# A four-phase graph network on one core: SyncE fetches one of 56 turns' rows in each GAT walk, and the index staging goes

## The reference, cut to what matters

```
def _gat_layer(x, src, dst, W, a_s, a_d, b, num_nodes):
    h = (x @ W).reshape(num_nodes, H, C)                     # H = 4, C = 32
    e = leaky_relu(alpha_src[src] + alpha_dst[dst], 0.2)
    e = exp(e - segment_max(e, dst)[dst])
    alpha = e / segment_sum(e, dst)[dst]
    return segment_sum(h[src] * alpha[:, :, None], dst) + b
```

## Time and profile before

| what | value |
|---|---|
| median of three runs | 6568.11 us |
| span of the profiled execution | 6570.3 us |
| VectorE busy | 4654.6 us, 71% |
| GpSimd busy | 4293.2 us, 65% |
| indirect gathers of rows (L725) | 3136, 2987.4 us busy |
| ScalarE busy | 1375.2 us, 21% |

### The profile page before, as it was taken

The page is one execution under the profiler, slowest core; times in us unless marked ns, Lnnn a source line. Parts: engine busy times, 40 slices in busy tenths (PEclk is TensorE's granted clock), DMA queues, the critical chain, the costliest instruction groups (busy, mean ns, idle before and its releaser), DMA issues. The chain is left out here.

```text
span 6570.3 us, 37158 instructions
## 1 busy us (share of the span) xinstructions
PE 1251.3 (19%) x8049; PEld 1094.3 (17%) x8049; DVE 4654.6 (71%) x9455; ACT 1375.2 (21%) x3580; POOL 4293.2 (65%) x4445
## 2 busy tenths in 40 slices
PE   7100000145555534332000000810000010000000
PEld 6100000135544433322000000610000010000000
DVE  7788888799999969987888887744444444444445
ACT  0122222220111114431000000622222211222223
POOL 0777777667777760027777775367777767777775
PEclk9555555555555555556555555955555555555555
DMA  9666666433443437754666664123333323333332
GB/s 391 199 218 202 202 199 204 130 106 131 132 136 133 133 115 292 295 184 153 220 219 218 225 218 158 30 85 109 113 111 109 115 74 90 112 113 109 113 111 82
DMA packets 338944, 1032.97 MB, mean 157 GB/s; under 512 B 100325, under 2 KB 163137, under 8 KB 331294
## 3 DMA queue, kind: packets, MB, share of 16 engines
q0 software_dynamic: 166752, 401.68, 21.4%
q1 hardware_dynamic: 116642, 342.34, 14.8%
q10 hardware_dynamic: 55324, 286.57, 12.1%
HBM read 602.97 MB, written 427.39 MB: 157 GB/s over the span
## 5 line engine op out<-in xcount | busy, mean ns | idle before, releaser
L725 POOL DMA_INDIRECT rows<-table,idx x3136 | 2987.4, 953 | 985.0 <-issue 973.1
L644 POOL DMA_INDIRECT by_src<-ebuf,place x784 | 767.4, 979 | 275.0 <-issue 238.3
L1296 DVE SCALAR_TENSOR_TENSOR psA<-psA,cont,dstf 128x128 f32<-128x128 f32 (+1 forms) x2349 | 836.6, 356 | 48.0 <-ACT ebuf L1025 27.2
L1285 DVE TENSOR_TENSOR sc<-rows,ebuf 128x56 f32<-128x56 f32 x112 | 28.2, 252 | 1023.9 <-DMA rows<-table,idx 1023.9
L958 PE MATMUL psA<-dstf,ones 128*128 128x512 f32 x10 | 9.9, 1113 | 3055.3 <-DVE dstf L2223 3055.3
L1296 DVE SCALAR_TENSOR_TENSOR sums<-sums,cont,psA 128x128 f32<-128x128 f32 (+1 forms) x1512 | 518.9, 343 | 30.3 <-ACT psA L1221 29.0
L958 PEld LDWEIGHTS psA<-dstf,ones 128*128 128x128 f32 x10 | 2.7, 317 | 3056.9 <-issue 3056.9
L823 PE MATMUL psA<-attr,sums 128*128 128x49 f32 x1568 | 406.1, 403 | 470.8 <-DVE attr L1475 470.8
L2104 DVE TENSOR_TENSOR_SCAN psA<-rows,psA 128x1980 f32<-128x1980 f32 x112 | 480.0, 4286 | 3.9
L823 PEld LDWEIGHTS psA<-attr,sums 128*128 128x128 f32 x1568 | 397.0, 326 | 476.9 <-DVE attr L1475 476.9
L1227 ACT ACTIVATE psA<-df 128x60 f32<-128x60 f32 (+1 forms) x168 | 40.4, 241 | 1714.2 <-DVE df L1285 1714.2
(11 more groups left out here) (350 smaller groups left out, 5533.6 us busy)
## 6 DMA issues: line engine op xcount, KB each, us to landing
dstf<-spread_wide SPq DMA_DIRECT2D x168, 924.0 KB
states<-sums ACTq DMA_DIRECT2D x150, 952.0 KB, 4.0
rows<-by_src SPq DMA_DIRECT2D x55, 1035.0 KB, 5.1
states<-sums ACTq DMA_DIRECT2D x56, 1008.0 KB, 5.7
spread_wide<-sums SPq DMA_DIRECT2D x56, 924.0 KB, 24.7
states<-sums ACTq DMA_DIRECT2D x56, 903.0 KB, 7.4
rows<-table,idx POOLq DMA_INDIRECT x3136
msg<-low_rows SPq DMA_DIRECT2D x56, 448.0 KB, 3.7
```

The source lines that it names most:

```text
L644: pool.indirect_dma_start(by_src[:, :], bass.IndirectOffsetOnAxis(ap=place[:, s, j:j + 1], axis=0), payload[:, s, j, :], None).then_inc(so ...
L725: pool.indirect_dma_start(rows[:, at:at + GW[ph]], None, table[ph][:, :], bass.IndirectOffsetOnAxis(ap=idx[:, s, j:j + 1], axis=0)).then_i ...
L1285: return dve.tensor_tensor(o_, a_, b_, op)
L1296: return dve.scalar_tensor_tensor(o_, a_, s_, b_, op0, op1)
```

## The change

In each GAT walk, turn 54 is left out of GpSimd's gathers. SyncE fetches its rows: for each of the 128 partitions it loads the 14 indices into registers, and for each index issues one copy of a single row of the table to its place in `msg`. VectorE reads turn 54 from `msg`, after a semaphore of its own. The other 55 turns of a GAT walk use the two slots of `rows` in turn, so turn 55 takes slot 0. In all four walks the staging of indices is gone: the gathers take their offsets from `src` directly, and POOL waits for `rows_used` alone.

```diff
+SIDE = {3: 54, 4: 54}
...
-        src = sb("src", [P, CH + 2 * B], I32)
+        src = sb("src", [P, CH], I32)
...
+        def row_slot(ph, g):
+            side = SIDE.get(ph, NG)
+            return None if g == side else (g - int(g > side)) % 2
+        def free_at(ph, g):
+            s = row_slot(ph, g)
+            users = [k for k in range(g) if row_slot(ph, k) == s]
+            return 2 + TURN[ph] * NG + (users[-1] + 1 if users else 0)
+        def turn_rows(ph, g):
+            s = row_slot(ph, g)
+            tile = msg[:, 0:B * GW[ph]] if s is None else rows[:, s * B * GW[ph]:(s + 1) * B * GW[ph]]
+            return tile.rearrange("p (b w) -> p b w", b=B)
...
+            def side_rows(ph):
+                w, at = GW[ph], SIDE[ph] * B
+                sp.wait_ge(src_in, 48)
+                sp.wait_ge(tab_saved, 16 * KG * TURN[ph])
+                sp.wait_ge(n_kept, 3 * KG)
+                for p in range(P):
+                    sp.load(numbers_of, src[p:p + 1, at:at + B])
+                    for j in range(B):
+                        node = sp.snap(numbers_of[j])
+                        sp.dma_start(msg[p:p + 1, j * w:(j + 1) * w], table[ph][bass.ds(node, 1), :]).then_inc(side_landed[ph], 16)
...
                 if ZW[ph] == 4:
                     sp.dma_start(dflat[:, 0:CH * 4], view.rearrange("p c d -> p (c d)")).then_inc(slim_in, 16)
+                    side_rows(ph)
...
-                            pool.wait_ge(idx_staged, g + (1 + TURN[ph] * (NG + 2)))
-                            pool.wait_ge(rows_used, g + (1 + TURN[ph] * NG))
+                        if s is None:
+                            continue
+                        pool.wait_ge(rows_used, free_at(ph, g))
...
-                                                        bass.IndirectOffsetOnAxis(ap=idx[:, s, j:j + 1], axis=0)).then_inc(rows_landed[s], 16)
+                                                    bass.IndirectOffsetOnAxis(ap=src[:, g * B + j:g * B + j + 1], axis=0)).then_inc(rows_landed[s], 16)
...
-                        act.wait_ge(rows_used, g + (3 + TURN[ph] * NG))
-                        act.activation(idx[:, s, :], src[:, bass.ds((g + 2) * B, B)], ACT.Copy).then_inc(idx_staged, 1)
...
-                        G3 = rows[:, s * B * GW[ph]:(s + 1) * B * GW[ph]].rearrange("p (b w) -> p b w", b=B)
+                        G3 = turn_rows(ph, g)
...
-                        dve.wait_ge(rows_landed[s], it * (16 * B) + (16 * B + TURN[ph] * IT * 16 * B))
+                        if row_slot(ph, g) is None:
+                            dve.wait_ge(side_landed[ph], 16 * B * P)
+                        else:
+                            dve.wait_ge(rows_landed[row_slot(ph, g)], landed_at(ph, g))
```

More of the change, by code:

```diff
@@ L125, in build @@
         attr = sb("attr", [P, 2, B * 32])
-        idx = sb("idx", [P, 2, B], I32)
         cg = sb("cg", [P, 2, B])
@@ L360, in build @@
         dve_step = sem("dve_step")
-        idx_staged = sem("idx_staged")
+        side_landed = {p: sem(f"side_landed{p}") for p in SIDE}
         rows_landed = [sem(f"rows_landed{s}") for s in range(2)]
@@ L439, in scattered_at, with slot_turns, landed_at @@
             return 16 * KB * (ph * turns + g // ZS + 1)
+        def row_slot(ph, g):
+            side = SIDE.get(ph, NG)
+            return None if g == side else (g - int(g > side)) % 2
+        def slot_turns(ph, s, g=NG):
+            return sum(row_slot(ph, k) == s for k in range(g))
+        def landed_at(ph, g):
+            s = row_slot(ph, g)
+            before = sum(slot_turns(q, s) for q in TURN if q < ph)
+            return 16 * B * (before + slot_turns(ph, s, g) + 1)
+        def free_at(ph, g):
[3 more added lines that the diff above has]
+        def turn_rows(ph, g):
+            s = row_slot(ph, g)
+            tile = msg[:, 0:B * GW[ph]] if s is None else rows[:, s * B * GW[ph]:(s + 1) * B * GW[ph]]
+            return tile.rearrange("p (b w) -> p b w", b=B)
         FIRST_LOADS = 6
@@ L545, in edge_features @@
                 sp.dma_start(attr[P - 1:P, s, :], attr_tail.rearrange("(p c) d -> p (c d)", p=1)[:, at]).then_inc(attr_landed[s], 16)
+            numbers_of = [sp.alloc_register(f"side_row{j}") for j in range(B)]
+            def side_rows(ph):
[8 more added lines that the diff above has]
+                        sp.dma_start(msg[p:p + 1, j * w:(j + 1) * w], table[ph][bass.ds(node, 1), :]).then_inc(side_landed[ph], 16)
             for ph in range(6):
@@ L715, in _ @@
                         pool.wait_ge(tab_saved, 16 * KG * TURN[ph])
-                    for it in range(IT):
-                        for s in range(2):
-                            g = it * 2 + s
-                            pool.wait_ge(idx_staged, g + (1 + TURN[ph] * (NG + 2)))
-                            pool.wait_ge(rows_used, g + (1 + TURN[ph] * NG))
[L721 to L725, removed]
-                                                        bass.IndirectOffsetOnAxis(ap=idx[:, s, j:j + 1], axis=0)).then_inc(rows_landed[s], 16)
+                    pool.wait_ge(src_in, 48)
+                    if ph:
+                        pool.wait_ge(n_kept, (2 if ph == 2 else 3) * KG)
+                    for g in range(NG):
+                        s = row_slot(ph, g)
+                        if s is None:
+                            continue
+                        pool.wait_ge(rows_used, free_at(ph, g))
+                        if g == 1 and ph < 3:
+                            spreads_landed()
+                        for j in range(B):
+                            at = (s * B + j) * GW[ph]
+                            pool.indirect_dma_start(rows[:, at:at + GW[ph]], None, table[ph][:, :],
+                                                    bass.IndirectOffsetOnAxis(ap=src[:, g * B + j:g * B + j + 1], axis=0)).then_inc(rows_landed[s], 16)
                     for s in range(2):
@@ L1197, in _ @@
                     sorted_pass()
[L1198 to L1201, removed]
                 def chain_gates(g):
```

## The result

The changed kernel takes 6655.4 us in the median of its runs (6652.9 to 6660.0), beside 6569.1 us (6567.3 to 6572.2) for the kernel before in the same comparison. The ratio is 1.0131 (95% interval 1.0116 to 1.0145): 86 us slower, where 6537 us was forecast. What happened is rival 1, SyncE too slow.

The account below looks back on a forecast made before the run. GAT walks were taken as bound by GpSimd's count of gathers. From 6568.1 us, 30.2 for the gathers left out and 1 for staging were subtracted, SyncE's work hidden: 6537 us, range 6530 to 6740.

Parts of the forecast that it names:

- rival 1: VectorE's wait ahead of turn 54: SyncE too slow, from 0.543 us a row; 6772 us at 0.60; chance 0.28.
- What bounds the kernel: GAT walks: bound by the number of indirect gathers GpSimd issues, 784 taking 742 us a walk; VectorE waits every turn.
- What is removed: End of each GAT walk: 14 gathers go, turn 54 follows at once in 10.30 us; 15.1 us saved, 30.2 in sum.
- The staging: ScalarE's index copies in all four walks: removal saves between 0 and 9.5 us, in phase 0; taken as 1 us.
- What is added: SyncE in GAT walks: 1792 single-row copies and 128 loads, 0.50 us a row, 896 us a walk, hidden, some 60 early.
- GpSimd's gap: GpSimd's queue between two gathers: 0.31 us of uncounted work; half, 0.15, taken for SyncE's register work per row.
- the budget: SyncE's time before VectorE wants turn 54: 957.7 us a walk over 1792 rows, 0.534 us a row.
- the upper bound of 0.31: SyncE's register work per row (load, move, address multiplication): at most GpSimd's 0.31 us between gathers, giving 0.69 us a row.
- The point of decision: SyncE's price of a row in a GAT walk: at 0.543 us the saving of 15.1 us is gone.
- The row's traffic: DMA in GAT walks: 14 more packets per partition against 784 don't lengthen the gathers; cost nothing.
- Rival 2: GAT walks: no change, a row costs 0.536 to 0.547 us or gathers stretch by 20 ns; about 6568 us; chance 0.06.
- rival 3: End of GAT walks: the full turn, 17.5 us a walk, is saved; 6532 us; within the forecast's own range, no separate chance.

Follow-up runs that it names:

- the run at fixed addresses: Changed kernel, all 14 columns by SyncE, without index loads or register arithmetic (rows fetched are not the graph's): 6552.2 us, 0.9950 of the kernel before.
- the kernel without a side turn: Changed kernel with no turn given to SyncE: GpSimd gathers all 56 turns, index staging stays away; 6584.2 us, 0.9996 of the kernel before.
- The run at 0.545: Changed kernel, all 14 columns by SyncE, indices laid out through DRAM so one load fills 32 registers: 6574.5 us, 1.0004 of the kernel before.
- the four changed kernels: Changed kernel with 7 columns; 32 registers a load; 13 columns of turn 52, 32 registers; turn 54 in first walk alone: 1.104, 1.201, 1.185, 1.107 of before.

## Why the prediction was wrong

- **What bounds the kernel: right.** A GAT walk follows the number of gathers until VectorE with ScalarE is the limit: 7 left out bring 9.5 us a walk, 12 or 14 of turn 54 bring 15.4, 13 of turn 52 bring 17.1.
- **What is removed: right, mechanism and size.** Turn 54 behind turn 53 without a wait, 10.2 us for a turn that follows at once (forecast 10.30), seen where the rows are in time. All 14 gathers left out, with the rows in time, is the run at fixed addresses: 2084.7 us over the scans of both walks (4355.8 to 6440.5), and 2114.8 (4357.3 to 6472.1) for the kernel without a side turn on the same chip. That is 30.1 us, where 30.2 were forecast.
- **The staging: right at nothing.** 0.9996 alone. The four waits of phase 0 that were 9.5 us for ScalarE's copy are still there as 7.6 us, for ScalarE's sums instead: 1.9 us was the copy's part.
- **What is added: wrong in one term, and this is the step that failed.** The text took 0.50 us a row: 0.30 for the copy, 0.05 to the next instruction, "and half of GpSimd's gap, 0.15, for the registers". Measured: 0.568, above the budget of 0.534. The copy and the gap behind it were cheaper than taken, 0.250 + 0.052 = 0.30 and not 0.35. The register work is 0.26 us and not 0.15: 0.118 for the load, 0.073 for arithmetic and move, 0.073 for the gaps behind these two. Its row was the wrong kind: GpSimd's 0.31 us lies between gathers and doesn't say what SyncE spends on a load of 14 registers; the upper bound of 0.31 did hold the truth, and halving it had no row behind it. And a gap of 0.05 was counted once, where a row has three instructions and so three gaps, 0.125 us.
- **An overlap put at nothing.** The text has no term for what the other engines' work does to SyncE's instructions, apart from taking the copy below its median. Of the 0.568 us, 0.036 come from instructions that are long behind ScalarE's save of the sums, 63 and 67 us a walk. Without them a row would take some 0.53 us, at the edge of the budget. The dearer register work alone would have eaten nearly the whole margin, and the long instructions carried the rows past it; that the save causes them is likely and not shown.
- **The point of decision: nearly right.** Text: 0.543 us. The account above gives 17.2 and not 15.1 us for nothing, because a late turn 54 no longer stands behind ScalarE's order: 957.7 + 17.2 over 1792 is 0.544. The run at 0.545 is 0.04% from no change. At 0.568 the text's own rule gives (0.568 - 0.534) x 1792 = 61 us late a walk, where 58.5 and 62.8 were traced, and 6537 + 2 x 61 = 6659 us, where 6655 were measured.
- **The row's traffic: right.** Gathers of 944 ns in the median and 947 in the mean, as before.
- **Rival 1 had the place, the price and the condition,** with a chance of 0.28, two thirds of it below 0.60 us a row, where the price fell. The text said of itself that the prediction fails above 0.19 us of register work, and called the margin 7%. The stated range holds 6655 us only because it was drawn up to 6740 for this rival; the forecast itself was a gain of 31 us, and there is a loss of 86. Rival 2's stretched gathers and rival 3's full turn at turn 54 aren't borne out; a nearly full turn appears only when turns follow behind it.
- **The two rules of the Trainium skill.** The Trainium skill, "DMA: Bandwidth & Descriptors", section "Why a DMA increments its semaphore by 16 and not by 1", has 512 cycles a copy for previous generations, from which the text estimated 0.43 us. The trace doesn't agree: 0.225 us in the median, and a copy every 0.32 us at fixed addresses. The Trainium skill, "Runtime: NRT & Kernel Launch", section "Instruction fetch mechanics", puts a register load at about 200 ns a register even in bulk. The traces have 173 ns for each of 7 registers (1.21 us), 104 for each of 14 (1.46 us) and 66 for each of 32 where the load didn't fall behind a save (2.1 us), so the rule is up to three times too high here. Its direction, that bulk loads aren't nearly free, was right. The estimate by it alone (0.55 us, 28 us late) was nearer than mine, but by luck: it has 0.20 for the load, where 0.118 was measured, and nothing for arithmetic, move and their gaps, 0.146 together.

## What to carry to other kernels

When an idle engine is to take a piece of another's work, build its time per item instruction by instruction, with a gap behind each, and price a register load by a measured load of that size. Leave a margin for what the other engines do to it: here 63 to 67 us a walk came on top, with instructions that were long once a turn. Where it has thousands of items and a margin of a few per cent, give it a little less than the whole piece: 12 of 14 columns brought as much as 14 would have. Give the helper its part early enough that the consumer has turns left to catch up. A helper that is early costs nothing, while one that is late costs its lateness less some 17 us in every walk here, so the cut should be on the early side.

## What the runs showed of the hardware

- SyncE with an address in a register: the copy of one row (544 bytes) took 225 ns in the median, 252 at a fixed address; the address arithmetic took 44 and the move 29, and 34 to 52 ns lay between two instructions. Such a loop took 0.45 us a row without loads, and 0.32 at fixed addresses.
- Once in every turn, between 0.4 and 3.5 us behind the start of ScalarE's DMA of the sums, SyncE's instructions were long: copies of 0.407 us in the mean beside 0.227 elsewhere, loads of 14 registers 2.31 us beside 1.46, loads of 32 registers 3.97 us beside 2.1.
- A register load on SyncE in a GAT walk took 1.03 us for 12 registers, 1.21 for 7 and 1.46 for 14 (medians), and 2.04 to 2.15 for 32 where it didn't fall behind a save. It took more for 7 than for 12, which I can't explain; the chips of these two runs differ, but 14 registers took 1.46 us on the chip of the 7 too. The row of the 7, and that of the 12:

```profile
L585 SPq TENSOR_LOAD <-src x256: 1082/1208/3277, 4325.0 to 6034.3; - x128
...
```

```profile
L585 SPq TENSOR_LOAD <-src x256: 909/1028/2774, 4323.7 to 6286.9; - x128
```

- Chips differ: the kernel before took 6569 and 6570 us in two sets of runs, 6588 on another chip and 7515 on one more, where the same copies of SyncE were 3.2 us apart beside working engines and 0.5 us apart beside idle ones. There the four changed kernels lost 10 to 20%, most of all those with the most rows on SyncE (1.20 with 3584, 1.19 with 3328, 1.10 and 1.11 with 1792).
